# Two attention layers and a mixture of experts in one kernel: first-layer weight pieces split on another engine and in another order, statistics buffers and four queue orders changed

## The reference

```python
x = x + xattn(layernorm(x), ctx, ...)      # self attention, cross attention, dense part
x = x + ffn(layernorm(x), ...)             # mixture of experts

def xattn(x, enc):                         # 16 heads of 64
    x = layernorm(x + attention(x, x, mask)) * ln1_g + ln1_b
    x = layernorm(x + attention(x, enc, mask)) * ln2_g + ln2_b
    h = gelu(x @ fc1_w + fc1_b)            # 256 -> 1024
    return layernorm(x + h @ fc2_w + fc2_b) * ln3_g + ln3_b

def ffn(x):                                # 8 experts, top 1, 256 -> 1024 -> 256
    shared = gelu(x @ w1s) * (x @ w2s) @ w3s
    e = argmax(x @ Wg)
    return shared + gelu(x @ W1[e]) * (x @ W2[e]) @ W3[e]
```

## Time and profile before

| | |
|---|---|
| median of three runs | 1245.56 us |
| profiled execution | 1244.36 us |
| its span, first to last instruction | 1242.6 us |
| TensorE busy | 1218.9 us, 98% |
| VectorE, ScalarE, GpSimd busy | 995.5, 875.4, 705.0 us |
| attention / dense / gated part, about | 0 to 779 / 779 to 881 / 881 to 1243 us |

### The profile page before, as it was taken

The page is one execution under the profiler, slowest core; times in us unless marked ns, Lnnn a source line. Parts: engine busy times, 40 slices in busy tenths (PEclk is TensorE's granted clock), DMA queues, the critical chain, the costliest instruction groups (busy, mean ns, idle before and its releaser), DMA issues.

```text
span 1242.6 us, 31390 instructions
## 1 busy us (share of the span) xinstructions
PE 1218.9 (98%) x10415; PEld 1165.9 (94%) x10415; DVE 995.5 (80%) x2685; ACT 875.4 (70%) x2261; POOL 705.0 (57%) x1100
## 2 busy tenths in 40 slices
PE   8899999999999999999999999899999999999998
PEld 6899999999999999999999999899999999999898
DVE  6898988988989988888888888754454888888964
ACT  5788887888888888878878877544333776777642
POOL 4676656656678856555555578876515222334451
PEclk9999999999999999999999999999999999999999
DMA  6060000000000003200000010010004677877722
GB/s 195 2 244 22 2 18 19 2 18 19 2 27 27 2 27 121 77 27 27 2 27 27 2 36 27 27 49 30 1 20 152 224 267 270 267 247 249 264 82 92
DMA packets 74383, 100.60 MB, mean 81 GB/s; under 512 B 5616, under 2 KB 53616, under 8 KB 74224
## 3 DMA queue, kind: packets, MB, share of 16 engines
q1 hardware_dynamic: 72688, 94.40, 23.1%
q0 software_dynamic: 1536, 4.20, 1.1%
HBM read 84.16 MB, written 14.42 MB: 79 GB/s over the span
## 4 chain that ended last, share of the span: by engine, by line
PE 78%; DVE 7%; ACT 5%; issue 4%; POOL 4%; DMA 1%; POOLq 0%; DVEq 0%; ACTq 0%
PE ps_pj L52 9%; PE ps_pj L54 9%; PE ps_pj L53 9%; PE ps_t L949 8%; PE ps_s L939 8%; PE ps_pv L962 8%; PE ps_aux L52 3%; PE ps_aux L54 3%; PE ps_aux L53 3%; ACT probs L1268 3%; PE ps_s L52 3%; PE ps_s L54 3%; PE ps_s L53 3%; PE ps_pv L54 2%; PE ps_pv L53 2%
## 5 line engine op out<-in xcount | busy, mean ns | idle before, releaser
L666 POOL TENSOR_SCALAR probs<-probs,inv 128x256 f32<-128x256 f32 x512 | 237.2, 483 | 224.1 <-DVE inv L1512 223.4
L1268 ACT ACTIVATE probs<-scores,nb 128x256 f32<-128x256 f32 x512 | 253.6, 497 | 18.4 <-DVE nb L1502 17.9
L1502 DVE CUSTOM_DVE_ANT_0 scores<-ps_s,maskf 128x256 f32<-128x256 f32 x512 | 186.8, 421 | 51.3 <-PE ps_s L939 49.2
L1275 ACT ACTIVATE probs_t_hi<-ps_t 128x512 fp32r<-128x512 f32 x256 | 150.8, 590 | 103.4 <-PE ps_t L949 103.4
L1516 DVE TENSOR_TENSOR probs_t_lo<-ps_t,probs_t_hi 128x512 fp32r<-128x512 f32 x256 | 173.1, 676 | 0.2
L949 PE MATMUL ps_t<-ident,probs 128*128 128x128 f32 x1024 | 139.9, 279 | 0.6 <-POOL probs L666 0.6
L962 PE MATMUL ps_pv<-probs_t_lo,v_stack 128*128 128x256 f32 x512 | 130.6, 287 | 0.8 <-issue 0.7
L962 PE MATMUL ps_pv<-probs_t_hi,v_stack 128*128 128x256 f32 x512 | 127.8, 282 | 0.0
L949 PEld LDWEIGHTS ps_t<-ident,probs 128*128 128x128 f32 x1024 | 109.7, 141 | 17.8 <-POOL probs L666 0.9
L52 PE MATMUL ps_pj<-xq_hi,wq_lo 128*128 128x256 f32 x368 | 115.3, 313 | 3.3 <-POOL wk_lo L713 3.2
L685 POOL TENSOR_TENSOR heads_t_lo<-joined,heads_t_hi 128x256 fp32r<-128x256 f32 x128 | 95.1, 743 | 33.4 <-ACT heads_t_hi L1284 33.0
(11 more groups left out here) (285 smaller groups left out, 4480.6 us busy)
## 6 DMA issues: line engine op xcount, KB each, us to landing
raw<-in_L_ffn_W SPq DMA_DIRECT2D x96, 512.0 KB, 4.7
slot_rows<-hin SPq DMA_DIRECT2D x3, 768.0 KB, 5.9
rows<-in_x SPq DMA_DIRECT2D x8, 256.0 KB, 2.7
after_self<-rows SPq DMA_DIRECT2D x8, 256.0 KB, 2.1
rows<-after_self SPq DMA_DIRECT2D x8, 256.0 KB, 2.8
cin<-in_ctx SPq DMA_DIRECT2D x8, 256.0 KB, 3.0
after_cross<-rows SPq DMA_DIRECT2D x8, 256.0 KB, 2.2
stage<-in_L_xattn_fc_w SPq DMA_DIRECT2D x2, 1024.0 KB, 9.3
```

Source lines behind the costliest of these rows:

```text
L666: last = pool.tensor_scalar(PR[:, h, t, :], PR[:, h, t, :], inv[:, h, t:t + 1], 1.0, ALU.mult, ALU.mult)
L1268: last = act.activation(PR[:, h, t, :], SM[:, h, t, :], ACT.Exp, bias=nb[:, h, t:t + 1], scale=-1.0, accum_out=sums[:, h, t:t + 1])
L1275: act.activation(flat(PT[0][:, i % 2, h, :, :]), ps_t[h][:, :], ACT.Copy).then_inc(t_hi, 1)
L1502: last = dve.tensor_tensor_reduce(SM[:, h, t, :], ps_s[h][:, t * S:(t + 1) * S], maskf[:, i // PAIRS % 2, :], -SCALE, -LOWEST, ALU.add, AL ...
```

## The change

- First layer: the high parts of the eleven later pieces go from VectorE to ScalarE (`first_high`, counted by a semaphore of its own). Three pieces (`AHEAD`: v1, q2, k2) are split before pair 0: ScalarE makes v1 after v0 and before the eviction of the first projection, q2 before the first exponentials, k2 after the eviction of v; GpSimd makes the low parts of v1 and q2 before the first division, that of k2 after it. The others move up by up to one iteration; in iteration i ScalarE makes them last.
- Opening: 14 warm matmuls instead of 17; GpSimd computes only the scale and mean of the first rows, and VectorE applies them between the first two low parts. `residual(0)` goes from pair 0 to pair 6.
- The step-1 transposes go ahead of the value product of pair 127. A third set of statistics buffers serves the dense part; `dense_stats(0)` no longer waits for turn 15. `affine_output(15)` goes behind `norm_second(2)`, its store behind four more loads on SyncE. `shared_lows` goes ahead of the first hidden chunk of step 1.
- Step 8: the parts of "l" 6 go from behind chunk 0 to behind the gate of chunk 1, on ScalarE and VectorE. `assign_slots` goes from step 10 to the end of step 9.

```diff
@@ -114,8 +114,8 @@
 BASES = (0, (B - 1) * PAIRS, (2 * B - 1) * PAIRS)
-PIECES_IN = [{0: [("v", 1), ("q", 2)], 1: [("k", 2), ("v", 2)], 2: [("o", 0)], 3: [("q", 3), ("k", 3)],
-              4: [("v", 3)], 5: [("o", 1)], 6: [("o", 2)], 7: [("o", 3)]},
+AHEAD = [("v", 1), ("q", 2), ("k", 2)]
+PIECES_IN = [{0: [("v", 2)], 1: [("q", 3), ("k", 3)], 2: [("o", 0)], 3: [("v", 3)], 4: [("o", 1)], 5: [("o", 2)], 6: [("o", 3)]},
              {0: [("q", 0)], 1: [("k", 0), ("v", 0)], 2: [("q", 1), ("k", 1)], 3: [("v", 1)],
@@ -130,7 +130,7 @@
-LATE = [(set_of(j), kind, q) for j in sorted(PIECES_AT) for kind, q in PIECES_AT[j]]
+LATE = [(0, kind, q) for kind, q in AHEAD] + [(set_of(j), kind, q) for j in sorted(PIECES_AT) for kind, q in PIECES_AT[j]]
 LATE_COUNT = {piece: n + 1 for n, piece in enumerate(LATE)}
@@ -143,7 +143,7 @@
 WPIECES = 2 * HALVES
-WARM, WARM_AFTER = 17, 6
+WARM, WARM_AFTER = 14, 6
@@ -313,8 +313,8 @@
         nb, sums, inv = (little(n, [P, 2, ST]) for n in ("nb", "sums", "inv"))
-        part, mv = little("part", [P, 2, ST, 6]), little("mv", [P, 2, ST, 2])
-        veps, rstd, nmean = (little(n, [P, 2, ST]) for n in ("veps", "rstd", "nmean"))
+        part, mv = little("part", [P, 3, ST, 6]), little("mv", [P, 3, ST, 2])
+        veps, rstd, nmean = (little(n, [P, 3, ST]) for n in ("veps", "rstd", "nmean"))
         b1 = little("b1", [P, FC])
@@ -367,6 +367,7 @@
         early_hi, early_lo, late_hi, late_lo = sem("early_hi"), sem("early_lo"), sem("late_hi"), sem("late_lo")
+        first_hi, first_scale = sem("first_hi"), sem("first_scale")
         x_in, y_stored = [sem(f"x_in{r}") for r in range(RING)], [sem(f"y_stored{r}") for r in range(RING)]
@@ -601,8 +602,9 @@
             load_x(1)
-            store(NTURN - 1)
             for n in range(3, DENSE):
+                if n == DENSE - 1:
+                    store(NTURN - 1)
                 load_h(n)
@@ -707,11 +709,18 @@
+            def late_low(layer, kind, q):
+                n = LATE_COUNT[(layer, kind, q)]
+                if layer == 0:
+                    pool.wait_ge(first_hi, n)
+                else:
+                    pool.wait_ge(late_hi, n - LATE_FIRST)
+                pool.tensor_tensor(piece(W[kind][1], 0, kind, q), raw_piece(kind, q),
+                                   piece(W[kind][0], 0, kind, q).bitcast(F32), ALU.subtract).then_inc(late_lo, 1)
+
             def split_late(i):
                 for kind, q in PIECES_AT.get(i, ()):
-                    pool.wait_ge(late_hi, LATE_COUNT[(set_of(i), kind, q)])
-                    pool.tensor_tensor(piece(W[kind][1], 0, kind, q), raw_piece(kind, q),
-                                       piece(W[kind][0], 0, kind, q).bitcast(F32), ALU.subtract).then_inc(late_lo, 1)
+                    late_low(set_of(i), kind, q)
@@ -730,7 +739,7 @@
                 pool.wait_ge(fstat_ready, n + 1)
-                link(norm_rows(1, h, h))
+                link(norm_rows(2, h, h))
                 link(pool.tensor_tensor(h, h, both(g3_b[:, :]), ALU.mult))
@@ -815,11 +824,17 @@
             pool.wait_ge(half_ready, 1)
-            norm_input(0)
+            pool.wait_ge(xstat_ready, 1)
+            link(pool.tensor_scalar(veps[:, 0, :], mv[:, 0, :, 1], EPS, 1.0, ALU.add, ALU.mult))
+            link(pool.tensor_scalar(nmean[:, 0, :], mv[:, 0, :, 0], -1.0, 0.0, ALU.mult, ALU.add))
+            pool.tensor_tensor(rstd[:, 0, :], veps[:, 0, :], mhalf[:, :], ALU.pow).then_inc(first_scale, 1)
             pool.wait_ge(mask_in, 16)
             build_mask(0)
+            late_low(0, *AHEAD[0])
+            late_low(0, *AHEAD[1])
             normalise(0, 0)
             normalise(0, 1)
+            late_low(0, *AHEAD[2])
             for i in range(NPAIR):
@@ -828,7 +843,7 @@
                 split_late(i)
-                if p == 0:
+                if p == (6 if u == 0 else 0):
                     residual(u)
@@ -847,7 +862,6 @@
             norm_output(NTURN - 1)
-            affine_output(NTURN - 1)
             for n in range(DENSE):
@@ -857,6 +871,8 @@
                 norm_second(n)
+                if n == 2:
+                    affine_output(NTURN - 1)
             count_tiles()
@@ -1185,11 +1201,12 @@
                     {"v": project_v, "xq": transpose_rows, "xc": transpose_ctx}[extra[0]](extra[1])
+                if i == NPAIR:
+                    transpose_step(1)
                 if 1 <= i <= NPAIR:
...
                     up_dense(0, i - NPAIR + 2)
-            transpose_step(1)
             down(0, range(FC))
@@ -1246,6 +1263,10 @@
+            def first_high(kind, q):
+                act.wait_ge(first_in[(kind, q)], 16)
+                act.activation(piece(W[kind][0], 0, kind, q), raw_piece(kind, q), ACT.Copy).then_inc(first_hi, 1)
+
             def hi_of_bank(what):
@@ -1297,13 +1318,16 @@
             early(2)
+            first_high(*AHEAD[0])
             hi_of_bank(("qk", 0))
...
             early(4)
+            first_high(*AHEAD[1])
             exps(0, 0)
...
             hi_of_bank(extra_event(-1))
+            first_high(*AHEAD[2])
             for i in range(NPAIR):
@@ -1330,6 +1354,9 @@
                     cross_of_pair(i - 1)
+                if i < PAIRS:
+                    for kind, q in PIECES_AT.get(i, ()):
+                        first_high(kind, q)
                 if i == 2 * PAIRS:
@@ -1413,13 +1440,13 @@
                 gelu_glu(step, 0)
-                if step == DENSE:
-                    hi_of_x(("l", step - 2))
                 if splits:
...
                     gelu_glu(step, j)
+                    if step == DENSE and j == 1:
+                        hi_of_x(("l", step - 2))
                     if splits:
@@ -1454,22 +1481,21 @@
                 base = BASES[layer]
+                if layer == 0:
+                    return
                 for kind, q in PIECES_AT.get(i, ()):
-                    if layer == 0:
-                        dve.wait_ge(first_in[(kind, q)], 16)
...
                    dve.tensor_copy(piece(W[kind][0], 0, kind, q), raw_piece(kind, q)).then_inc(late_hi, 1)
...
                 for kind, q in SHARED_PIECES:
-                    dve.wait_ge(late_hi, LATE_COUNT[(2, kind, q)])
+                    dve.wait_ge(late_hi, LATE_COUNT[(2, kind, q)] - LATE_FIRST)
                     dve.tensor_tensor(piece(W[kind][1], 0, kind, q), raw_piece(kind, q), piece(W[kind][0], 0, kind, q).bitcast(F32),
@@ -1613,11 +1639,8 @@
                 dve.wait_ge(y_done, n + 1)
-                if n == 0:
-                    dve.wait_ge(y_ready, NTURN)
-                else:
-                    dve.wait_ge(x2_ready, n)
-                row_stats(1, hin[:, n % 3, :, :], fstat_ready)
+                wait(dve, x2_ready, n)
+                row_stats(2, hin[:, n % 3, :, :], fstat_ready)
@@ -1681,6 +1704,10 @@
             early(0)
+            dve.wait_ge(first_scale, 1)
+            for t in range(ST):
+                last = dve.tensor_scalar(rows[0][:, t, :], rows[0][:, t, :], nmean[:, 0, t:t + 1], rstd[:, 0, t:t + 1], ALU.add, ALU.mult)
+            last.then_inc(qrow_ready, 1)
             early(1)
@@ -1742,10 +1769,10 @@
                         lo_of_x(("l", step - 2))
+                    if step == 1:
+                        shared_lows()
                     if step >= 1:
                         lo_of_hidden(step, 0)
-                    if step == 1:
-                        shared_lows()
                     for j in range(1, HP):
@@ -1784,17 +1811,15 @@
                 gate(step, 0)
-                if step == DENSE:
-                    lo_of_x(("l", step - 2))
                 if step == DENSE + 1:
                     choose()
-                if step == DENSE + 2:
-                    assign_slots()
                 if splits:
...
                     gate(step, j)
+                    if step == DENSE and j == 1:
+                        lo_of_x(("l", step - 2))
                     if j == 1 and is_single(step - 1):
@@ -1808,6 +1833,8 @@
                     lo_of_x(("l", DENSE - 1))
+                if step == DENSE + 1:
+                    assign_slots()
                 if step == DENSE + FRONT + SLOTS:
```

More of the change, by code:

```diff
@@ L1456, in late_hi_pieces @@
                 base = BASES[layer]
+                if layer == 0:
+                    return
                 for kind, q in PIECES_AT.get(i, ()):
-                    if layer == 0:
-                        dve.wait_ge(first_in[(kind, q)], 16)
-                    else:
-                        dve.wait_ge((second_in, third_in)[layer - 1][kind], 16)
-                        if kind == "o":
-                            dve.wait_ge(out_done, base + 2 * (q + 1))
-                        elif kind == "v":
-                            dve.wait_ge(pj_done, EVENT[("v", base // 2 + q)] + 1)
-                        else:
-                            dve.wait_ge(pj_done, EVENT[("qk", base + 2 * q + 1)] + 1)
+                    dve.wait_ge((second_in, third_in)[layer - 1][kind], 16)
```

(6 more changed lines are left out.)

## The result

The changed kernel takes **1231.51 us** (median of 4 runs, 1231.06 to 1232.08), the kernel before 1245.82 (4 runs, 1244.93 to 1246.37): ratio 0.9886, 95% interval 0.9869 to 0.9903. The profiled execution of after took 1231.06 with a span of 1229.3; that of before 1244.36 and 1242.6, so 13.3 us between the two profiles and 14.3 between the medians. The forecast was 1233.6.

The account below looks back on a forecast made before the run. TensorE, busy 98%, was taken as the bound, with only its waits and low-clock time to win. Nine terms summed to -11.95 us: profiled 1244.36 to 1232.4, plus 1.2 for the median, 1233.6; range 1230.8 to 1238.2.

Parts of the forecast that it names:

- rival (b): Clock falls in the opening's TensorE idle from 11.8 us, or still at 25 us: +1.4 each, 1235 to 1236.4; chance 0.20.
- The step from profile to median: From the profiled execution's forecast, 1232.4, to the median's, 1233.6: 1.2 added, as before's median lay 1.2 above its profile.
- Part 1: Opening, 0 to 15 us: faster first rows swallowed by ScalarE waiting for v1's load: +0.4, bounds -1.0 and +0.6.
- Part 2: Pairs 0 to 5, 15 to 50 us: -1.8 from VectorE's chain, -3.1 for pair 4's gap, -1.4 for its clock fall.
- ceiling of 2.7: Most that the -1.8 gain in pairs 0 to 3 could reach: wait and clock, 1.3 + 1.4.
- Part 3: Dense entry, 770 to 804 us: transposes -0.35, low parts ahead of hidden(1,1) -1.5, router normalisation -2.0.
- Rival (a): Near 800 us GpSimd's normalisation steps each wait for a whole VectorE operation: +2.4, 1236.0; chance 0.10.
- Part 4: Routing, 880 to 930 us: l6 parts behind chunk 1's gate -0.7, assign_slots earlier -1.5.
- (c): Opening: v1 lands before 10.6 us: -1.4, 1232.2; chance 0.10.
- (d): Turn 0: ScalarE, given 11 more pieces, becomes the bound and the kernel is slower; chance 0.02.
- (e): First 50 us: the opening and pair edits don't do what they say, another input being as late: 1239.5; chance 0.03.
- two of the signs that were named: Signs of being right: TensorE's waits under 9 us; first projection's eviction at 12.3 behind a ScalarE DMA wait.

Follow-up runs that it names:

- before_fill: The kernel before with 24 matmuls, their result overwritten, in TensorE's wait for low k3 in pair 4: 1244.16 us.
- front_old: The changed kernel with the whole front (first-layer pieces, casts, residual, first rows) as in the kernel before, dense and routing edits kept: 1235.96 us.
- rows_first: As v1_behind, and VectorE normalises the first rows before its first low part: 1231.10 us.
- pool_rows: The changed kernel with the first rows normalised on GpSimd again: 1233.33 us.
- l6_back: The changed kernel with the splits of block 6 at dense step 8 ahead of the second half again: 1233.62 us.
- after_again: The changed kernel, unchanged, run and profiled once more: 1232.05 us.
- casts_on_dve: The changed kernel with the high parts of the eight later first-layer pieces (v2 to o3) on VectorE again: 1232.46 us.
- assign_back: The changed kernel with the slots assigned one step later again, at the old place in VectorE's order: 1233.93 us.
- shared_stats: The changed kernel with dense statistics sharing the output's buffers again, turn 15's affine and store back, shared low parts behind hidden(1,0) again: 1235.59 us.
- before_again: The kernel before, unchanged, run and profiled once more: 1245.49 us.
- v1_behind: The changed kernel with the high part of v1 behind the eviction of the first projection on ScalarE: 1231.49 us.

## Why the prediction was right, point by point

**The clock.** The granted clock is at 1.00 from 0 to 60 us in the trace of after. One term was -1.4 for the fall behind the wait in pair 4; it measured 1.36, and before_fill shows the same size. (The forecast's "lose 15 or 16 starts" means that 15 or 16 matmuls start in the stretch, each 0.09 us later than at full clock.) What the forecast didn't see is that a fall differs from execution to execution: front_old has the 2.9 us wait and no fall, and rows_first, pool_rows and l6_back have a fall between 33 and 38 us, behind waits of 1.0 and 0.64, with 1.5 to 1.6 lost each (rows_first from pair 3 to pair 5: 1.54). That is rival (b), in another place than its 11.8 or 25 us. In the two runs of the changed kernel it is one execution of eight (1233.60). So the gain has two parts: executions at mean clock 1.000 have medians of 1243.4 before (seven) and 1231.8 after (seven), 11.6 us from closed waits, and the rest, some 2 to 3 us of the 14.3, is that before nearly always falls at least once and after rarely. before has three places for it, near 26, 46 and 805 us.

**The step from profile to median** is where more than a third of the error lies. The forecast added 1.2 since before's profiled execution lay 1.2 under its median. But before's spread is that of its falls, and after has few: its median is 0.45 over its profile. That step was wrong by 0.75 of 2.1 us.

**Part 1 was mis-sized and had the wrong sign**: +0.4 forecast, -0.25 in these two traces. Over six traces with after's opening (after, after_again, casts_on_dve, l6_back, assign_back, shared_stats) the first exp starts at 14.64 to 15.43, mean 15.09; over four with before's (before, before_again, before_fill, front_old) at 15.18 to 15.66, mean 15.49: -0.4. Of that the transposes, at 7.48 instead of 8.24, give -0.76 (forecast -1.0), and the stretch from there to the first exp costs +0.35 (forecast +1.4). The mechanism was right (ScalarE waits for v1 ahead of its eviction) and its input was one execution's landing at 11.8; in the seven traces of kernels with v1 ahead of the eviction it is used at 10.75 to 11.71. Against that the transposes started at 7.38, not at 6.9, because GpSimd's nmean took 0.66: a collision in the opening that the forecast placed only near 800 us. The trace that the forecast was read from doesn't show it, since q0 landed later there than in any other (split at 4.95) and the low part began at 5.61, behind nmean; before_again has nmean at 0.61. The two errors, the landing and the collision, partly cancel; v1_behind and rows_first show each alone.

**Part 2 held.** -1.8 and -4.5 are the measured numbers. casts_on_dve gives 1.2 of the 1.8 to the casts, and the rest goes with the v1 wait. The first fall adds nothing, though the forecast had it in its ceiling of 2.7: from pair 0 to 3 before and before_again, with the fall at 25 to 30 us, lose 1.79 and 1.69 against after, before_fill and front_old, without it, 1.70 and 1.71. It is paid inside the next wait, for the low part of k at 32 us, which is 0.27 and 0.20 us with the fall and 1.28 without. What was late next in pair 3 is listed as a wait of 1.0 for issue at 31.67. It is the join that the forecast named (32.2 in its steps): VectorE ends it at 31.57, and the value product starts 0.1 later here and in six other traces. From 33.6 to 126 us TensorE has no idle spell over 0.12 us. Not forecast: 0.65 comes back between 100 and 180 us, where the score product waits 0.43 and 0.46 (0.11 and 0.12 before) for the low q,k part that ScalarE and VectorE make late:

```profile
127.31 0.39 PE L955 MATMUL ps_s<-qk_hi,qk_lo 64*128 64x256 f32 x2 [0.43 <-DVE qk_lo L1510]
```

The table shows it for every version against the old fronts (6.58 to 5.93, 5.61 to 4.92, 5.60 to 4.90), and hardly among the new ones. Which edit does it wasn't tried and stays open.

**Part 3 held**, with a little more in it: -1.55 and -2.3 for -1.5 and -2.0. The statistics run at 780.26 (forecast 785.9 in before's time, 780.0 with the 5.9 won in parts 1 and 2 taken off), the shared low parts end at 783.7, ahead of hidden(1,0). Rival (a), a collision in place of the wait, didn't come: GpSimd's router normalisation takes 3.43 us as before, and starts early enough.

```profile
790.19 0.51 POOL L673 TENSOR_SCALAR veps<-mv 128x2 f32<-128x2 f32 x1
790.79 0.51 POOL L674 TENSOR_SCALAR nmean<-mv 128x2 f32<-128x2 f32 x1
791.39 1.03 POOL L675 TENSOR_TENSOR rstd<-veps,mhalf 128x2 f32<-128x2 f32 x1
792.52 1.09 POOL L677 TENSOR_SCALAR stage<-stage,nmean,rstd 128x256 f32<-128x256 f32 x2
...
793.83 0.27 PE L1000 MATMUL ps_t<-ident,stage 128*128 128x128 f32 x1
```

Two of VectorE's four low parts of w3 beside it:

```profile
789.06 1.59 DVE L1791 TENSOR_TENSOR probs_t_lo<-raw,probs_t_hi 128x512 fp32r<-128x512 f32 x1
...
790.57 0.68 DVE L1791 TENSOR_TENSOR probs_t_lo<-raw,probs_t_hi 128x512 fp32r<-128x512 f32 x1
```

The normalisation ends at 793.6 and the transposes follow at 793.83 without a wait. The forecast had 0.1 left, since it let GpSimd begin 0.4 us later than it did (796.5 less 5.9 is 790.6, and it began at 790.19). Rival (a) counted a whole 0.7 us for each small step. They take 0.3 more each, because each begins some 0.2 us into a low part of VectorE, and ends 0.05 us behind it (791.30, the low part 791.25).

**Part 4 held**: -0.85 and -1.55; l6_back and assign_back bring back 0.84 and 1.56. (The 0.59 of l6 is the middle one of the three waits in the earlier trace rows, not the smaller; that is 0.43, at the last output.)

**The end.** -0.65 was not forecast and isn't the change's. In before TensorE lost 0.6 us (listed as 0.43) at the last output, as VectorE waited 2.27 us for gathered rows. Of the other thirteen traces assign_back and v1_behind have 0.17 and 0.19 there, the rest, before_again among them, nothing: it belongs to the execution. This -0.65 and the +0.65 of the layers, both unforeseen, cancel in the total, which is luck.

**The other rivals.** (c): v1 never landed before 10.6. (d): ScalarE, 5.4 us busier, doesn't become the bound: TensorE has no idle spell over 0.12 us in the rest of turn 0. (e): both parts did what they say. And two of the signs that were named failed: TensorE's listed waits are 11.8 us, not under 9 (5.8 on low q,k parts instead of 4.0, 1.2 on the first rows, 1.0 on issue), and the first eviction came at 11.58, not at 12.3.

## What to carry to other kernels

Price each idle spell of the bounding engine by itself, step the queue of the engine that feeds it, and name what is late next: eight of the nine terms came out within 0.3 us this way. Take a landing or a clock fall from one trace as one draw; where the kernel's own executions spread over 4 us, look first at which of them have the full clock, and forecast the two kinds apart. Ask of a fall what is late behind it: in front of another wait it cost nothing here. An instruction that waits for a load should stand behind everything in its queue that doesn't need it, and short fills in the waits of an opening may buy a steadier clock: here they delayed nothing, and four of four executions had it.

## What the runs showed of the hardware

- **VectorE against GpSimd.** A GpSimd step of 128x2 took 0.19 us alone and 0.58 to 0.71 in the ten traces where a 0.69 us VectorE low part with two SBUF inputs had begun just before it (in after 4.90 to 5.59; the step ends at 5.65). The Trainium skill, "SBUF — State Buffer", section "Who interferes with whom", says that such a pair excludes each other for a whole instruction; here the step ended 0.06 us behind the low part, and this row agrees. Near 790 us so do both sides: the first of the four w3 low parts starts beside a 128x512 step of GpSimd and takes 1.59 us, the other three 0.68 as usual, and GpSimd's steps between them take 0.51 instead of 0.19, ending 0.05 us behind the low part they began beside. One row doesn't fit: in before the rstd step (5.29 to 6.03) and the low part that begins during it (5.61 to 6.30) both keep their lengths.
- **Landings.** The same 256 KB load of v1, issued at 4.36 or 4.37, landed at 10.73 to 11.72 in the fourteen traces, 1.0 us apart, with no order by kernel. The first weight piece was used at 4.24 to 4.95.
- **The clock.** Each of the eight stretches at 1.2 GHz in these traces lasts 3.4 us. It costs 1.3 to 1.6 us where TensorE is what the others wait for, and at most 0.1 at 25 us, ahead of a wait. It came behind idle spells of 1.0 and 0.6 us, and in front_old stayed away behind one of 2.9; of 39 executions with after's waits in pairs 1 to 3 (in casts_on_dve longer ones), 28 had a mean clock of 1.000, of 47 of before seven, and with those waits filled four of four.
